# Cross-attention keys produced already turned, with their head norms applied to the scores

## The chip, the cores and the metric

The kernel runs on one core of a Trainium2 chip. The metric is the time of one execution in microseconds, the median of three runs. TensorE (PE) multiplies and turns tiles and writes PSUM; VectorE (DVE) and ScalarE (ACT) work on PSUM and SBUF; GpSimd (POOL) works on SBUF only; SyncE (SP) issues most transfers. The engines run their own instruction streams in order and meet through semaphores.

## The reference, cut to what matters

One block of a perceiver: cross-attention, a second attention without softmax, a mixture of experts. Only the cross-attention is touched. There are 32 sequences of 32 queries and 257 context rows, width 512, 8 heads of 64.

```
q = heads(layernorm(x) @ Wq);  k, v = heads(context @ Wkv)
q = per_head_ln(q) * qn_w;     k = per_head_ln(k) * kn_w     # (t-mean)*rsqrt(var+1e-6), over the head's 64
attn = softmax(where(mask, q @ k^T / 8, -inf));  out = (attn @ v) @ Wo
```

The kernel takes the mean out of the weights (each head's columns are centred), so a head norm is one multiply by rsqrt(mean of squares + eps). Both norm weights and the 1/8 are put on the queries.

## The kernel before, in words

**Precision.** A fp32 product is made of three fp32r products: both operands are split into a high part (ScalarE copy) and a low part (difference), and `split_products` (L23) issues high x high, high x low, low x high for each of 4 chunks of 128 of the contraction. All these matmuls carry the line L32.

**The loop.** `batch` (one in each engine's program) is one step b = 1 to 32, run in a register loop over tiles of 4 steps (r = 0 to 3). Step b finishes sequence b-1 and prepares b and b+1. The order on every engine is written out by hand. TensorE in step b:

1. scores of sequence b-1 (L1682): 8 products, keys of one head (64 rows) by 32 queries, on eight different 64x32 tiles of the array, into pS (2 banks);
2. turns of context b+1 (L1539), 8 transposes into the banks pT0 and pT1 (`pTT`);
3. second half of the keys of b: `k_half`, 12 products of 512 columns into pK1. The stationary operand is the turned context of 128 rows, so keys come out with a context row per partition;
4. the output tile of the last four sequences (L1638), in steps with r = 1 only, from step 5 on;
5. first half of the keys of b+1 into pK0, first 9 of its 12 products;
6. turns of the probabilities of b-1 (L1712), then the last 3 products of 5; with r = 0 also the turns of the last context row's probabilities (L1720);
7. turns of the normalised keys of b (L1730), 8 transposes into the same banks as 2;
8. products of context and probabilities (24 of 256 columns, into pP, then pV1; in the trace pP and pV by L32). Values are never made: the probabilities are applied to the context, and the weights come in 4.

VectorE in step b: masked scores (L1153, `s_m`), their maximum (L1156), the two low parts of context b+1 (L1033), four small operations for the softmax's divisor (L1164 to L1172), sum of squares and normalising of key half 1 (`k_sum` L1038, `k_norm` L1044), the low part of the turned probabilities (L1183), the last key column (L1190), the copy of turned keys (L1083), sum and normalising of the next key half 0, and the z copy (L1199).

ScalarE in step b: high part of context b (L768), high parts of the turned context b+1 (L668), two exponentials (L776), square of key half 1 (L676), scaling of the probabilities (L783), `k_root` (a Ln and an Exp of 8 columns, L680, L682), high part of the turned probabilities (L794), copy of turned keys (L672), square of the next half 0, a z copy (L814), again `k_root`; with r = 0 also four copies for the last row (L821).

GpSimd makes the context's low part (L541) and copies the queries (L547), in steps 30 and 31 also a low part of the attention output (L578). SyncE loads the context two steps ahead.

In front of the loop, eight query tiles are made; the keys of sequence 0 and half of those of 1 are made among them and after them, then the value product of the last context rows (L1623).

Of the kernel before, what the change touches and what calls it, by code (L numbers as in the profile page):

```python
# [15 lines left out]
P = 128  # L16
# [20 lines left out]
def perceiver_block(nc, x, ctx, mask, xWq, xWkv, xWo, qn_w, kn_w, aWq, gq, bq, mq, vq, aWk, gk, bk, mk, vk,  # L37
# [34 lines left out]
    with ExitStack() as es:  # L72
# [18 lines left out]
        def sem(name):  # L91
# [65 lines left out]
        kn_x = at("kn_x", [P, 3, D], 82 * KB)  # L157
# [9 lines left out]
        kn = at("kn", [P, 2, D], 113 * KB + 8320)  # L167
        p_rem = at("p_rem", [P, G, 3, B], 117 * KB + 8320)
# [104 lines left out]
        k_mm, k_sq, k_ss, k_lg, k_rs, k_n, k_t, kT0_set, kT1_set, k_rem = (sem(n) for n in (  # L273
            "k_mm", "k_sq", "k_ss", "k_lg", "k_rs", "k_n", "k_t", "kT0_set", "kT1_set", "k_rem"))
# [88 lines left out]


# [4 lines left out]
        def _(sp):  # L369
# [59 lines left out]
            sp.wait_ge(k_t, B * MT)  # L429
# [213 lines left out]
        def _(act):  # L643
# [26 lines left out]
            def keys_copy(n):  # L670
                act.wait_ge(k_t, (n - 1) * MT + 1)
                act.activation(kT[:, :, 0:P], pTT[0][:, :, :], ACT.Copy).then_inc(kT0_set, 1)  # L672

            def k_square(b, t):
                act.wait_ge(k_mm, b * MT + t + 1)
                act.activation(sq[:, t], pKV[t][:, :], ACT.Square).then_inc(k_sq, 1)  # L676
# [26 lines left out]
            for t in range(TILES):  # L703
# [38 lines left out]
                if t in (6, 7):  # L742
                    n = t - 6
                    act.wait_ge(k_mm, n + 1)
                    act.activation(sq_x[:, :], pC[1 - n], ACT.Square).then_inc(k_sq, 1)
                    act.wait_ge(k_ss, n + 1)
                    act.activation(head_log[:, 2], head_ss[:, 2], ACT.Ln, bias=HEAD_B, scale=1.0 / HD).then_inc(k_lg, 1)
                    act.wait_ge(k_lg, n + 1)
                    if n == 0:
                        act.wait_ge(rem_dve, 2)  # L750
                    else:
                        act.wait_ge(k_n, 1)
                    act.activation(head_rs[:, 2], head_log[:, 2], ACT.Exp, scale=-0.5).then_inc(k_rs, 1)
                if t == TILES - 1:
                    act.wait_ge(rem_pe, 3)
                    act.activation(kT_rem[:, :, :], pAV[0][:, :, 0:B], ACT.Copy).then_inc(rem_act, 1)
                    keys_copy(1)
            k_square(1, 0)
            k_root(1, 0)

            def batch(tile, r, main=True, prev=True, nxt=True, first=False):
# [25 lines left out]
                if main:  # L787
                    k_root(b, 1)
# [13 lines left out]
                if main:  # L802
                    keys_copy(b + 1)
# [11 lines left out]
                if nxt:  # L815
                    k_root(b + 1, 0)
# [179 lines left out]
        def _(dve):  # L996
# [39 lines left out]
            def k_sum(b, t):  # L1036
                dve.wait_ge(k_sq, b * MT + t + 1)
                nc.vector.tensor_reduce(head_ss[:, t], heads(sq[:, t]), AX.X, ALU.add).then_inc(k_ss, 1)  # L1038

            def k_norm(b, t, reused=True):  # L1040
                dve.wait_ge(k_rs, b * MT + t + 1)
                if reused:
                    dve.wait_ge(k_t, b * MT + t - 1)
                tt(heads(kn[:, t]), heads(pKV[t][:, :]), per_head(head_rs[:, t]), ALU.mult).then_inc(k_n, 1)  # L1044

# [35 lines left out]
            def keys_copy(n):  # L1081
                dve.wait_ge(k_t, n * MT)
# [891 lines left out]
```

## Time and profile before

| | us |
|---|---|
| median of 3 runs | 746.81 (746.39 to 746.88) |
| the profiled execution | 746.33 |
| its span, first to last instruction | 744.5 |
| TensorE busy | 712.8 (96%) |
| TensorE weight loads | 591.7 (79%) |
| VectorE busy | 490.5 (66%) |
| ScalarE busy | 441.3 (59%) |
| GpSimd busy | 239.4 (32%) |

The granted TensorE clock is 0.994 of full speed over the span. Busy times overlap. A TensorE row's length holds the modelled end of its last product; the pace is read from start to start. In the timeline a row may merge several instructions of one kind (xN); an entry in brackets says how long the engine stood idle before, and for whom.

### The profile page before, as it was taken

The numbers are of one execution on the slowest core, as the hardware profiler recorded it, in microseconds if no ns is written. First come the engines' busy times: TensorE is split into PE (matmuls) and PEld (weight loads), VectorE is DVE, ScalarE is ACT, GpSimd is POOL, SyncE is SP. The second block draws the span as 40 slices with busy tenths as digits, with TensorE's granted clock in tenths as the row PEclk, the third lists the DMA queues.
The fourth block names the chain that finished last, engine by engine and source line by source line (L and its number), as shares of the span: only waits on it lengthen the run. The fifth ranks groups of instructions, "written<-read, shape, count | busy, mean of one in ns | idle before, by whom it ended". The sixth has DMA issues, their size and how long they took to land.

```text
span 744.5 us, 14137 instructions
## 1 busy us (share of the span) xinstructions
PE 712.8 (96%) x4901; PEld 591.7 (79%) x4901; DVE 490.5 (66%) x903; ACT 441.3 (59%) x958; POOL 239.4 (32%) x208
## 2 busy tenths in 40 slices
PE   4899999999999999999999999999999969999995
PEld 3677888888888888888888888788778847888874
DVE  6766776775756757757667676867367875655573
ACT  4655775675766656756657675564655335655650
POOL 1462211221211212221212143753830023555525
PEclk9999999999999999999999999999999999999998
DMA  9931121212121212112212305630115447665658
GB/s 303 104 129 42 44 87 44 85 42 71 55 85 42 85 42 84 43 58 69 84 43 85 100 2 167 201 119 38 58 48 200 136 171 238 112 103 105 111 83 322
DMA packets 59672, 75.21 MB, mean 101 GB/s; under 512 B 8784, under 2 KB 33360, under 8 KB 59632
## 3 DMA queue, kind: packets, MB, share of 16 engines
q1 hardware_dynamic: 52032, 58.16, 26.0%
q0 software_dynamic: 4720, 11.27, 8.2%
q10 hardware_dynamic: 2880, 5.24, 2.0%
q8 instruction: 24, 0.39, 0.2%
q14 instruction: 16, 0.13, 0.1%
HBM read 54.75 MB, written 19.92 MB: 100 GB/s over the span
## 4 chain that ended last, share of the span: by engine, by line
PE 85%; DVE 6%; DMA 3%; ACT 2%; issue 2%; POOL 1%; SPq 0%; POOLq 0%; DVEq 0%
PE pK L32 41%; PE pV L32 11%; PE pP L32 9%; PE pV L1638 5%; PE pT L1539 4%; PE pT L1730 4%; PE pS L1682 2%; PE pP L1712 2%; PE pT L1877 1%; DMA fin<-total 1%; PE pT L1519 1%; DMA big<-x_rows,idx_x 1%; PE pS L1807 1%; DMA total<-big,idx 1%; PE pS L1900 1%
## 5 line engine op out<-in xcount | busy, mean ns | idle before, releaser
L32 PE MATMUL pK<-parts 128*128 128x512 f32 x744 | 187.8, 399 | 0.0
L541 POOL TENSOR_TENSOR parts<-big,parts 128x1024 fp32r<-128x1024 f32 x32 | 77.9, 2434 | 309.3 <-ACT parts L768 309.3
L32 PEld LDWEIGHTS pK<-parts 128*128 128x128 f32 x744 | 134.4, 188 | 27.0 <-issue 1.2
L1044 DVE TENSOR_TENSOR kn<-pK,head_rs 128x512 f32<-128x512 f32 x62 | 42.9, 692 | 58.0 <-ACT head_rs L682 58.0
L32 PE MATMUL pK<-w,lhs 128*128 x276 | 69.2, 399 | 0.9 <-issue 0.5
L32 PEld LDWEIGHTS pK<-w,lhs 128*128 128x128 f32 x276 | 50.3, 188 | 12.2 <-issue 2.5
L1465 DVE TENSOR_TENSOR w_p<-big,w_p 128x1024 fp32r<-128x1024 f32 x22 | 27.0, 1225 | 37.7 <-ACT w_p L959 37.7
L32 PE MATMUL pP<-pT,parts 128*128 128x256 f32 x384 | 51.6, 283 | 0.1
L616 POOL DMA_INDIRECT big<-x_rows,idx_x x23 | 26.7, 1162 | 73.7 <-DVE idx_x L1421 59.4
L1038 DVE TENSOR_REDUCE head_ss<-sq 128x8 f32<-128x512 f32 x62 | 42.5, 685 | 11.4 <-ACT sq L676 11.4
L676 ACT ACTIVATE sq<-pK 128x512 f32<-128x512 f32 x62 | 36.8, 594 | 21.4 <-PE pK L32 21.3
L32 PEld LDWEIGHTS pP<-pT,parts 128*128 128x128 f32 x384 | 46.3, 188 | 3.8 <-issue 1.8
L32 PE MATMUL pV<-pT,parts 128*128 128x256 f32 x384 | 49.1, 277 | 0.0
L794 ACT ACTIVATE pT<-pP 128x512 fp32r<-128x512 f32 x32 | 19.1, 598 | 48.9 <-PE pP L1712 48.8
L32 PE MATMUL pK<-w_p,parts 128*128 128x512 f32 x168 | 44.1, 412 | 3.7 <-DVE parts L1017 3.3
L32 PEld LDWEIGHTS pV<-pT,parts 128*128 128x128 f32 x384 | 46.2, 188 | 0.0
L622 POOL DMA_INDIRECT total<-big,idx x20 | 31.7, 1586 | 41.1 <-ACT big L973 41.1
L1183 DVE TENSOR_TENSOR pT<-pP,pT 128x512 fp32r<-128x512 f32 x32 | 22.1, 692 | 30.5 <-ACT pT L794 30.5
L32 PEld LDWEIGHTS pK<-w_p,parts 128*128 128x128 f32 x168 | 31.7, 195 | 12.2 <-DVE parts L1017 4.1
L1033 DVE TENSOR_TENSOR parts<-pT,parts 128x512 fp32r<-128x512 f32 x62 | 39.7, 681 | 2.2 <-ACT parts L668 2.2
L32 PE MATMUL pK<-w_a,xT_hi 128*128 128x512 f32 x128 | 40.1, 395 | 0.0
L768 ACT ACTIVATE parts<-big 128x1024 fp32r<-128x1024 f32 x31 | 32.7, 1053 | 6.6 <-PE pV L32 6.6
(330 smaller groups left out, 1523.0 us busy)
## 6 DMA issues: line engine op xcount, KB each, us to landing
big<-in_ctx_dram SPq DMA_DIRECT2D x32, 512.0 KB, 3.9
total<-zero SPq DMA_DIRECT2D x32, 256.0 KB, 4.1
w_raw<-in_L_ffn_w_dram SPq DMA_DIRECT2D x16, 512.0 KB, 6.1
big<-in_L_ffn_w_dram SPq DMA_DIRECT2D x8, 512.0 KB, 4.0
fin<-total SPq DMA_DIRECT2D x8, 512.0 KB, 7.8
x_rows<-big ACTq DMA_DIRECT2D x8, 256.0 KB, 2.1
total<-big ACTq DMA_DIRECT2D x8, 256.0 KB, 2.3
big<-in_x_dram SPq DMA_DIRECT2D x1, 1536.0 KB, 10.2
```

Of the source, the lines that this page charges most:

```text
L32: last = pe.matmul(out, lhs(a, c), rhs(b, c), start=start and c == first and n == 0, stop=stop and c == chunks - 1 and n == 2)
L541: nc.gpsimd.tensor_tensor(ctxN[:, u, LO], ctx_raw[:, u], ctxN[:, u, HI].bitcast(F32), ALU.subtract).then_inc(cn_lo, 1)
L622: nc.gpsimd.indirect_dma_start(total[:, :], bass.IndirectOffsetOnAxis(idx[:, j:j + 1], 0), y_sb[:, j % 2, :], None, bounds_check=5 * T - 1 ...
L676: act.activation(sq[:, t], pKV[t][:, :], ACT.Square).then_inc(k_sq, 1)
L768: act.activation(ctxN[:, u, HI], ctx_raw[:, u], ACT.Copy).then_inc(cn_hi, 1)
L1033: tt(ctxT[:, u, LO, :, t * P:(t + 1) * P], pTT[t][:, :, :], ctxT[:, u, HI, :, t * P:(t + 1) * P].bitcast(F32), ALU.subtract).then_inc(ctx_ ...
L1038: nc.vector.tensor_reduce(head_ss[:, t], heads(sq[:, t]), AX.X, ALU.add).then_inc(k_ss, 1)
L1044: tt(heads(kn[:, t]), heads(pKV[t][:, :]), per_head(head_rs[:, t]), ALU.mult).then_inc(k_n, 1)
L1465: tt(w2_buf(j)[:, LO], w2_all[:, bass.ds(e, 1)].rearrange("p e c n -> p (e c) n"), w2_buf(j)[:, HI].bitcast(F32), ALU.subtract).then_inc(w ...
L1539: last = pe.transpose(pTT[t][:, c, :], ctx_raw[:, u, t, c * P:(c + 1) * P], ident[:, :])
L1638: last = pe.matmul(o, weights, rows[:, e * C + c].rearrange("p b q -> p (b q)"), start=k == 0, stop=k == C, tile_position=(0, e * HD))
L1730: last = pe.transpose(pTT[t][:, c, :], kn[:, t, c * P:(c + 1) * P], ident[:, :])
```

## The change

The keys' product is turned round: a chunk of 128 weight columns is the stationary operand, all 256 turned context rows move. The keys come out with the head's dimension on the partitions, as the scores need them: half 0 (heads' chunks 0 and 1) in pK0, half 1 in pK1. They are copied to kT without norm. Their squares are multiplied by ones (which hold 1/512) on the tiles of the scores; this puts each head's mean of squares into pS where the scores will be, per query row and key. ScalarE makes the roots, `key_rs`, and VectorE multiplies the scores by them before the mask. The last context row's keys keep their old way. `k_sum`, `k_norm` and the key turns go.

```diff
+        key_rs = at("key_rs", [P, G, MT * P], 113 * KB + 8320)
+        half_keys = lambda buf, h: buf.rearrange("p (j m) -> p j m", j=2)
...
-            sp.wait_ge(k_t, B * MT)
             sp.wait_ge(p_t, B)
@@ ScalarE @@
-            def k_root(b, t):
-                act.wait_ge(k_ss, b * MT + t + 1)
-                act.activation(head_log[:, t], head_ss[:, t], ACT.Ln, bias=HEAD_B, scale=1.0 / HD).then_inc(k_lg, 1)
-                act.wait_ge(k_lg, b * MT + t + 1)
-                act.activation(head_rs[:, t], head_log[:, t], ACT.Exp, scale=-0.5).then_inc(k_rs, 1)
+            def keys_copy(b, src):
+                act.activation(kT[:, 0:2, 0:MT * P], half_keys(src, 0), ACT.Copy).then_inc(kT0_set, 1)
+            def k_square(b, h):
+                act.wait_ge(k_mm, b * 2 + h + 1)
+                act.wait_ge(ss_mm, b)
+                act.activation(sq[:, h], pKV[h][:, :], ACT.Square).then_inc(k_sq, 1)
+            def k_root(b, used=True):
+                act.wait_ge(ss_mm, b + 1)
+                if used:
+                    act.wait_ge(sc_s, b)
+                act.activation(key_rs[:, :, :], pS[:, :, 0:MT * P], ACT.Ln, bias=HEAD_B, scale=float(D // HD)).then_inc(ss_lg, 1)
+                act.wait_ge(ss_lg, b + 1)
+                act.activation(key_rs[:, :, :], key_rs[:, :, :], ACT.Exp, scale=-0.5).then_inc(k_rs, 1)
@@ ScalarE, batch @@
                     act.activation(ctxN[:, u, HI], ctx_raw[:, u], ACT.Copy).then_inc(cn_hi, 1)
+                    act.wait_ge(sc_mm, b)
+                    act.wait_ge(k_mm, b * 2 + 1)
+                    keys_copy(b, pKV[0][:, :])
                 if nxt:
                     ctx_high(b + 1, 1 - u)
...
-                if main:
-                    k_root(b, 1)
...
                 if main:
-                    keys_copy(b + 1)
+                    k_root(b)
                 if nxt:
                     k_square(b + 1, 0)
...
-                if nxt:
-                    k_root(b + 1, 0)
@@ VectorE, batch @@
                 if prev:
                     dve.wait_ge(sc_mm, b)
+                    dve.wait_ge(k_rs, b)
+                    tt(pS[:, :, 0:MT * P], pS[:, :, 0:MT * P], key_rs[:, :, :], ALU.mult).then_inc(sc_s, 1)
+                    dve.wait_ge(sc_s, b)
                     stt(s_m[:, :, 0:M], masked[:, bass.ds(p, 1), :].broadcast_to([P, G, M]), -BIG,
...
                 if main:
-                    k_sum(b, 1)
+                    dve.wait_ge(sc_mm, b)
+                    ts(kT[:, :, M - 1:M], kT_rem[:, :, bass.ds(b, 1)], 1.0, None, ALU.mult).then_inc(k_rem, 1)
+                    dve.wait_ge(k_sq, b * 2 + 2)
+                    keys_copy(pKV[1][:, :])
...
-                if main:
-                    k_norm(b, 1, reused=not first)
...
-                if main:
-                    dve.wait_ge(k_t, b * MT + 1)
-                    ts(kT[:, :, M - 1:M], kT_rem[:, :, bass.ds(b, 1)], 1.0, None, ALU.mult).then_inc(k_rem, 1)
-                    keys_copy(b + 1)
-                if nxt:
-                    k_sum(b + 1, 0)
-                if nxt:
-                    k_norm(b + 1, 0)
@@ TensorE @@
+            def key_products(bank, h, j, u, **part):
+                c = 2 * h + j
+                return split_products(pe, half_keys(bank, h)[:, j, :], weight(wkv, c * P, (c + 1) * P),
+                                      lambda s, k: ctxT[:, u, s, k, :], part.pop("chunks", C), **part)
+            def key_sums(b, squares):
+                pe.wait_ge(k_sq, b * 2 + 2)
+                pe.nop(nofuse=True)
+                for c in range(C):
+                    for e in range(2):
+                        half = slice(e * HD, (e + 1) * HD)
+                        last = pe.matmul(pS[c * S:(c + 1) * S, e, 0:MT * P], ones[half, 0:S],
+                                         half_keys(squares[half, c // 2, :], c // 2)[:, c % 2, :], start=True, stop=True,
+                                         tile_position=(e * HD, c * S))
+                last.then_inc(ss_mm, 1)
@@ TensorE, in front of the loop @@
-            pe.wait_ge(ctx_lo, 3)
-            key_turn(0)
-            split_products(pe, pK0[:, :], ctx_rows(1, 0), wk, C).then_inc(k_mm, 1)
-            pe.wait_ge(k_n, 2)
-            pe.wait_ge(ctx_lo, 4)
-            key_turn(1)
-            query_turn(TILES - 1)
+            query_turn(TILES - 1)
+            pe.wait_ge(ctx_lo, 4)
+            for j in range(2):
+                last = key_products(pK0[:, :], 0, j, 1)
+            last.then_inc(k_mm, 1)
+            pe.wait_ge(q_out, TILES)
+            key_sums(0, sq_first)
+            pe.wait_ge(kT1_set, 1)
@@ TensorE, batch @@
-                    if not first:
-                        pe.wait_ge(sc_m, b - 1)
+                    pe.wait_ge(ss_lg, b)
...
                 if main:
-                    pe.wait_ge(k_n, b * MT)
+                    pe.wait_ge(kT1_set, b)
+                    pe.wait_ge(k_sq, b * 2)
...
-                    k_half(b, 1, u)
+                    for j in range(2):
+                        last = key_products(pK1[:, :], 1, j, u)
+                    last.then_inc(k_mm, 1)
...
+                if main:
+                    pe.wait_ge(kT0_set, b + 1)
+                    pe.wait_ge(k_sq, b * 2 + 1)
                 if nxt:
-                    pe.wait_ge(k_n, b * MT + 1)
-                    pe.wait_ge(ctx_lo, b * MT + 3)
-                    split_products(pe, pK0[:, :], ctx_rows(1 - u, 0), wk, C - 1, stop=False)
+                    pe.wait_ge(ctx_lo, b * MT + 4)
+                    key_products(pK0[:, :], 0, 0, 1 - u)
+                    key_products(pK0[:, :], 0, 1, 1 - u, chunks=2, stop=False)
...
                 if nxt:
-                    split_products(pe, pK0[:, :], ctx_rows(1 - u, 0), wk, C, start=False, first=C - 1).then_inc(k_mm, 1)
+                    key_products(pK0[:, :], 0, 1, 1 - u, start=False, first=2).then_inc(k_mm, 1)
...
                 if main:
-                    pe.wait_ge(k_n, b * MT + 2)
...
-                    for t in range(MT):
-                        for c in range(C):
-                            last = pe.transpose(pTT[t][:, c, :], kn[:, t, c * P:(c + 1) * P], ident[:, :])
-                        last.then_inc(k_t, 1)
+                    pe.wait_ge(sc_m, b)
+                    key_sums(b, sq)
```

## Rows read from the trace of the kernel before

**Rows 1.** The page: busy us, share, instructions; the chain by line.
```profile
PE 712.8 (96%) x4901; PEld 591.7 (79%) x4901; DVE 490.5 (66%) x903; ACT 441.3 (59%) x958; POOL 239.4 (32%) x208
...
PE pK L32 41%; PE pV L32 11%; PE pP L32 9%; PE pV L1638 5%; PE pT L1539 4%; PE pT L1730 4%; PE pS L1682 2%; PE pP L1712 2%; PE pT L1877 1%; DMA fin<-total 1%; PE pT L1519 1%; DMA big<-x_rows,idx_x 1%; PE pS L1807 1%; DMA total<-big,idx 1%; PE pS L1900 1%
```

**Rows 2.** Timeline of TensorE in step 19: start us, length us, what.
```profile
290.00 0.66 PE L1682 MATMUL pS<-kT,q_b 64*32 64x257 f32 x16
290.59 1.09 PE L1539 MATMUL pT<-ident,big 128*128 128x128 f32 x8
291.44 5.05 PE L32 MATMUL pK<-parts 128*128 128x512 f32 x21
296.33 0.60 PE L1712 MATMUL pP<-ident,prob 128*128 128x128 f32 x4
...
297.46 1.04 PE L1730 MATMUL pT<-ident,kn 128*128 128x128 f32 x8
298.44 1.60 PE L32 MATMUL pP<-pT,parts 128*128 128x256 f32 x12
...
301.33 0.67 PE L1682 MATMUL pS<-kT,q_b 64*32 64x257 f32 x16
```

**Rows 3.** Timelines of TensorE in very short windows of the same step.
```profile
292.22 0.62 PE L32 MATMUL pK<-parts 128*128 128x512 f32 x2
...
295.88 0.62 PE L32 MATMUL pK<-parts 128*128 128x512 f32 x2
...
298.63 0.39 PE L32 MATMUL pP<-pT,parts 128*128 128x256 f32 x2
...
299.76 0.28 PE L32 MATMUL pP<-pT,parts 128*128 128x256 f32 x1
```

**Rows 4.** Timeline of VectorE and ScalarE in the same step.
```profile
289.84 0.69 DVE L1044 TENSOR_TENSOR kn<-pK,head_rs 128x512 f32<-128x512 f32 x1 [1.37 <-ACT head_rs L682]
...
290.45 0.68 DVE L1199 TENSOR_SCALAR z<-pV 128x512 f32<-128x512 f32 x1
...
291.05 0.68 DVE L1153 SCALAR_TENSOR_TENSOR s_m<-mask_f,pS 128x514 f32<-128x514 f32 x1
...
291.77 0.69 DVE L1156 TENSOR_REDUCE neg_max<-s_m 128x2 f32<-128x514 f32 x1
292.37 1.28 DVE L1033 TENSOR_TENSOR parts<-pT,parts 128x512 fp32r<-128x512 f32 x2
...
294.49 0.60 ACT L676 ACTIVATE sq<-pK 128x512 f32<-128x512 f32 x1 [0.90 <-PE pK L32]
294.98 0.90 ACT L783 ACTIVATE prob<-prob,p_scale 128x256 f32<-128x256 f32 x2
...
296.97 0.60 ACT L794 ACTIVATE pT<-pP 128x512 fp32r<-128x512 f32 x1 [0.59 <-PE pP L1712]
...
297.60 0.69 DVE L1183 TENSOR_TENSOR pT<-pP,pT 128x512 fp32r<-128x512 f32 x1 [0.49 <-ACT pT L794]
```

**Rows 5.** Timeline at the start of step 1 and of step 32.
```profile
66.35 0.67 PE L1682 MATMUL pS<-kT,q_b 64*32 64x257 f32 x16
...
67.19 0.69 DVE L1153 SCALAR_TENSOR_TENSOR s_m<-mask_f,pS 128x514 f32<-128x514 uint8 x1 [1.35 <-PE pS L1682]
...
451.72 0.66 PE L1682 MATMUL pS<-kT,q_b 64*32 64x257 f32 x16
...
451.82 0.69 DVE L1199 TENSOR_SCALAR z<-pV 128x512 f32<-128x512 f32 x1 [2.46 <-PE pV L32]
...
452.49 0.69 DVE L1153 SCALAR_TENSOR_TENSOR s_m<-mask_f,pS 128x514 f32<-128x514 uint8 x1
```

**Rows 6.** Timeline of GpSimd and VectorE in step 31.
```profile
444.07 1.30 POOL L578 TENSOR_TENSOR out_first<-qoT,out_first 128x512 fp32r<-128x512 f32 x1
...
444.42 0.97 DVE L1168 SCALAR_TENSOR_TENSOR p_scale<-neg_max,p_inv 128x2 f32<-128x2 f32 x1
```

**Rows 7.** Groups by line: a Ln of 512 columns: busy us, mean ns.
```profile
L826 ACT ACTIVATE bn_vec<-bn_vec,bias 128x512 f32<-128x512 f32 x2 | 1.4, 720 | 0.3 <-DMA bn_vec<-in_L_attn_vq_dram 0.3
```

More of the change, by code:

```diff
@@ L272, in perceiver_block @@
         ctx_t, ctx_hi, ctx_lo = sem("ctx_t"), sem("ctx_hi"), sem("ctx_lo")
[L273 to L274 removed]
+        k_mm, k_sq, ss_mm, ss_lg, k_rs, sc_s, kT0_set, kT1_set, k_rem = (sem(n) for n in (
+            "k_mm", "k_sq", "ss_mm", "ss_lg", "k_rs", "sc_s", "kT0_set", "kT1_set", "k_rem"))
         cn_hi, cn_lo = sem("cn_hi"), sem("cn_lo")
@@ L744, in _ @@
                     act.wait_ge(k_mm, n + 1)
[L745 to L748, printed above, removed]
+                    act.activation(sq_first[:, n], pC[1 - n], ACT.Square).then_inc(k_sq, 1)
                     if n == 0:
[L750 to L753, printed above, removed]
+                        keys_copy(0, pC[1])
                 if t == TILES - 1:
@@ L1597, in _ @@
                     pe.wait_ge(ctx_lo, 2)
-                    split_products(pe, pC[1], ctx_rows(0, 0), wk, C).then_inc(k_mm, 1)
+                    for j in range(2):
+                        last = key_products(pC[1], 0, j, 0)
+                    last.then_inc(k_mm, 1)
                 if t == 7:
@@ L1687, in batch @@
                 if main:
-                    pe.wait_ge(k_n, b * MT)
+                    pe.wait_ge(kT1_set, b)
+                    pe.wait_ge(k_sq, b * 2)
                     if first:
                         pe.wait_ge(q_n, TILES)
-                    k_half(b, 1, u)
+                    for j in range(2):
+                        last = key_products(pK1[:, :], 1, j, u)
+                    last.then_inc(k_mm, 1)
                 if r == 1 and not first:
                     out_tile(tile - 1)
+                if main:
+                    pe.wait_ge(kT0_set, b + 1)
+                    pe.wait_ge(k_sq, b * 2 + 1)
                 if nxt:
-                    pe.wait_ge(k_n, b * MT + 1)
-                    pe.wait_ge(ctx_lo, b * MT + 3)
-                    split_products(pe, pK0[:, :], ctx_rows(1 - u, 0), wk, C - 1, stop=False)
+                    pe.wait_ge(ctx_lo, b * MT + 4)
+                    key_products(pK0[:, :], 0, 0, 1 - u)
+                    key_products(pK0[:, :], 0, 1, 1 - u, chunks=2, stop=False)
                 if main and not nxt:
-                    pe.wait_ge(k_n, b * MT + 1)
                     project(0)
@@ L1724, in batch @@
                 if main:
-                    pe.wait_ge(k_n, b * MT + 2)
-                    if nxt:
-                        pe.wait_ge(ctx_lo, b * MT + 4)
-                    for t in range(MT):
-                        for c in range(C):
-                            last = pe.transpose(pTT[t][:, c, :], kn[:, t, c * P:(c + 1) * P], ident[:, :])
-                        last.then_inc(k_t, 1)
+                    pe.wait_ge(sc_m, b)
+                    key_sums(b, sq)
                 if prev:
```

58 lines of the change are left out of this document (15 added, 43 removed).

## The prediction

> **What bounds the kernel now.** I read three views in this order: the page's busy times and chain, the timeline of TensorE inside the cross-attention loop, and then the other engines in the same stretch. TensorE is busy 712.8 us of 744.5, and the chain of work that ended last runs through its products; the two lines that write pK, pV and pP lead it [rows 1]. So time is TensorE's program order plus what it waits for. A step of the loop (steps b = 1 to 32 score sequence b-1) repeats almost unchanged; rows 2 show step 19, from S = 290.00 to the next S at 301.33, 11.33 us. Its parts: scores 0.59, context turns 0.85, 21 key products 4.89, turns of the probabilities at T = S+6.33, 3 key products, 8 key turns, then the products of probabilities and context at T+2.11 until the next S, 2.89.
>
> The key turns start at 297.46 and would take what the 8 context turns take, 0.85; the next products start 0.98 later [rows 2]. They were waiting for a chain: T at 296.33, ScalarE's high part at 296.97, VectorE's low part at 297.60 for 0.69, TensorE at 298.44, so 0.15 from the end of that write to the product [rows 2, 4]. So T to T+2.11 is set by the other engines, and TensorE work removed there gives nothing. Before T, TensorE is the bound: ScalarE's scaling of the probabilities ends at 295.88, 0.45 before T [rows 4].
>
> **Key products, 24 of 512 columns become 48 of 256.** The order turns round (weights as stationary operand, turned context moving), so keys come out turned. Price from one stretch: the 4th product of 512 starts at 292.22 and the 20th at 295.88, 16 steps of 0.229. The 2nd of 256 columns starts at 298.63 and the 12th at 299.76, 10 steps of 0.113 [rows 3]. Two of 256 cost 0.226, a hair less than one of 512. Before T: 42 x 0.113 + 0.08 for the first (0.19 between first and second, 298.44 to 298.63) = 4.83 against 4.89, -0.06. The lower end of this cost is that -0.06, the upper end the mean over a whole block of them (298.44 to 301.33 is 24 in 2.89, 0.120 each [rows 2]), 42 x 0.120 + 0.08 = 5.12, +0.23. I take 0.113, since a block's excess sits in its first and last steps. The last 6 of the 48 lie behind T, where the chain hides them.
>
> The Trainium skill (TensorE: Matmul & The Clock Gate, section Back-to-back issue gap) gives a warm matmul N/2.4 ns plus a fixed 2.5 ns. By that, 24 more of them would cost an estimated 0.06 per step where the rows give -0.06. The rows decide, but a size rule that speaks against the change is kept as a rival.
>
> **Key turns out, sums of squares in.** The 8 turns go; 8 products of squares with ones come, on the same eight 64x32 tiles as the scores, one column fewer: 0.59 [rows 2]. Behind T TensorE now has 0.36 + 6 x 0.113 + 0.59 = 1.63 before the chain lets it go at 2.11: gain 0, and 0.48 of cover. Should the sums not run side by side on their tiles as the scores do (ends: 0.59 and 16 passes x 0.113 = 1.8, as each of the 8 shows two records), the excess over 0.48 would be 0.7 per step.
>
> **VectorE.** Per step, two reductions and two normalising multiplies go (one is the 0.69 at 289.84 [rows 4]); a copy of keys stays the same size and moves forward; one multiply of 128x512 of scores by the roots comes, PSUM in and PSUM out. Busy time falls about 4 x 0.69 - 0.69 = 2.1 us per step, off the chain. But the new multiply stands first in VectorE's queue, in front of mask, maximum and the two context low parts. And TensorE now wants both low parts for the next step's first key product, since a turned product spans all 256 rows; before, it wanted the first only. This is the step that decides, so I lay it out from S:
> - z copy: before, it started at S+0.45 because the normalising multiply held VectorE [rows 4]; with that gone it starts when the products end, S+0.10 to 0.15 (451.72 to 451.82, VectorE idle [rows 5]). The scores are readable at S+0.84 (66.35 to 67.19) or S+0.77 (451.72 to 452.49, behind the z copy) [rows 5]: multiply at S+0.80.
> - multiply to mask: a waited successor follows at 0.72 (291.05 to 291.77 [rows 4]). No row shows VectorE writing PSUM; ends 0.65 and 0.85, I take 0.74, nearest to the operations that read PSUM. Mask S+1.54, maximum 2.26, first low part 0.60 later 2.86, both end 1.28 later at 4.14, TensorE 0.15 later: S+4.29.
> - TensorE is free at 1.44 + 24 x 0.113 + 0.08 = S+4.23 (S to 291.44 is 1.44).
> So about 0.06 of new wait, and some of the 0.08 that a first product takes: 0.11 of stall against 0.06 gained, +0.05 per step. Ends: ready at 4.20, no stall, -0.06; ready at 4.45, +0.24.
>
> The Trainium skill (Perfetto Trace Analysis, section Optimizing Scalar/DVE Operations) puts VectorE's access overhead near 60 ns in SBUF and 125 ns in PSUM. By that, a PSUM destination would put the multiply's successor an estimated 0.06 later than the rows' 0.72. No row here shows it.
>
> **ScalarE.** Four 8-column roots per step become a Ln and an Exp of 512; such a Ln takes 0.72 [rows 7], Exp at most that. They run after the high part: sums end near T+1.65, Ln by T+2.6, Exp by T+3.3; the scores that wait for the Ln start at T+5.0, the multiply that waits for the Exp later still. Hidden, with 2.4 to spare. Its copy of the first key half goes in front of the context high parts and delays them by at most a copy's 0.60 (296.97); the low parts now come 0.5 later themselves. The exponentials end 1.13 after the maximum now (maximum to 292.46, ScalarE idle for 0.90 before 294.49), so at S+4.1 after the change; the square that stands behind them waits for the second key half and starts at S+4.49 as now, so the scaling ends at S+5.88 as now, under T [rows 4]. GpSimd's parts keep their place; SP's dropped wait for key turns precedes one for the probability turns that comes later, so it moves no load.
>
> **The ends.** Steps 30 and 31 are different: there GpSimd computes low parts of the output (444.07, 1.30 us) and a small VectorE operation stands still until they end (444.42, 0.97 us [rows 6]). The two in front of it now get through before; with VectorE's chain 0.5 later all three queue behind it, 0.5 later, and the slack of 0.3 under T goes: +0.35 each, +0.7. At the front, two groups of 4 turns go (-0.85), the sums come (+0.59), three key blocks save 0.04 each: -0.3; the roots lie behind the value product of the last row.
>
> **Sum.** 22 steps with r = 0, 2 or 3: 22 x 0.05 = +1.1. The 8 steps with r = 1 have the output tile (or, in step 1, a free VectorE) as cover: 8 x -0.06 = -0.5. Ends +0.7 - 0.3 = +0.4. Together +1.0 on the profiled execution of 746.33 (its span is 744.5, 1.8 lie around it and stay), 747.3; the median of the runs, 746.81, is 0.48 above it, so 747.8 as a median. A change is measurable here from about 0.2%, 1.5 us: I forecast no measurable change.
>
> **Rivals.**
> 1. The context low parts decide (slower). If the multiply cannot start before S+1.05, where the mask starts now, all of VectorE's chain is 0.25 later, ready is 4.54, the stall 0.31 + 0.08, and 22 x 0.33 + 0.4 - 0.5 = +7: 754. It decides from ready = S+4.3; each 0.1 costs 2.2. For it: 0.06 of nominal stall is already there. Against: what holds VectorE until S+0.45 is removed. Chance 0.30, most of it with halfway values, 749 to 752.
> 2. No stall (faster). Ready under 4.23: 30 x -0.06 - 0.3, with or without the ends' 0.7: 744.7 to 745.4. For it: margins within the rows' own scatter. Chance 0.22.
> 3. Smaller products cost more each. At the 0.120 of whole groups, TensorE is free at 4.40, which hides the stall; 22 x 0.23 + 8 x 0.2 + 0.4 = +7: 754; half of it, 750. Against it: ten even steps of 0.113. Chance 0.07.
> 4. The sums run one after the other on their tiles: 31 x 0.7 = +22, 768. The scores on the same tiles speak against it. Chance 0.02.
> Forecast, within 1.5 us of 746.8: 0.39.
>
> **How the numbers follow.** Time 747.8. The range leaves out rival 4, the top of 1 and 3 and little below: 744.4 to 753.0. Faster 0.22, same 0.39, slower 0.39.
>
> **What would show it.** Right: the 21-product block becomes 42 in about 4.83 plus a gap of 0.1 after the 24th; T to the next product stays 2.1; VectorE's busy time falls by some 65 us with no gain in span. Wrong: the multiply of scores starts later than S+0.9 or holds the mask longer than 0.8; a product of 256 columns steps at more than 0.115; the sums take over 1.1; the interval from S to S leaves 11.2 to 11.5.

## The result and the profile after

The changed kernel takes 756.27 us in the median of 4 runs (754.61 to 757.34) beside 746.85 for the kernel before on the same chip: 1.0114 times as long, 95% interval 1.0093 to 1.0134. The prediction was 747.8, within 744.4 to 753.0, and no measurable change: the kernel is slower by 9.4 and lies outside the range. The profiled execution took 755.76, its span 754.0, 9.5 more than the 744.5 of before.

First the page: busy times, the chain by line, and two groups. They answer to [rows 1].

```profile
PE 717.9 (95%) x5925; PEld 617.3 (82%) x5925; DVE 426.6 (57%) x807; ACT 447.3 (59%) x894; POOL 239.6 (32%) x208
...
PE 80%; DVE 9%; ACT 4%; DMA 3%; issue 2%; POOL 0%; SPq 0%; POOLq 0%; DVEq 0%; ACTq 0%
...
L32 PE MATMUL pK<-parts 128*128 128x256 f32 x1488 | 195.4, 287 | 0.9 <-DVE parts L1032 0.9
...
L1167 DVE TENSOR_TENSOR pT<-pP,pT 128x512 fp32r<-128x512 f32 x32 | 22.1, 691 | 64.4 <-ACT pT L795 64.4
```

VectorE lost 63.9 us of work and the span grew all the same. The 1488 key products waited for VectorE 0.9 us in the whole execution, all of it in step 4 (below), so for the rest their own pace or TensorE's order is the place to look, not a stall.

Next the timeline of TensorE in step 19, which answers to [rows 2].

```profile
295.52 0.67 PE L1665 MATMUL pS<-kT,q_b 64*32 64x257 f32 x16
296.11 1.09 PE L1516 MATMUL pT<-ident,big 128*128 128x128 f32 x8
296.96 5.28 PE L32 MATMUL pK<-parts 128*128 128x256 f32 x42
302.07 0.60 PE L1700 MATMUL pP<-ident,prob 128*128 128x128 f32 x4
302.43 0.96 PE L32 MATMUL pK<-parts 128*128 128x256 f32 x6
303.32 0.66 PE L1525 MATMUL pS<-sq,ones 64*32 64x256 f32 x16
304.18 1.60 PE L32 MATMUL pP<-pT,parts 128*128 128x256 f32 x12 [0.20 <-DVE pT L1167]
305.62 1.52 PE L32 MATMUL pV<-pT,parts 128*128 128x256 f32 x12
307.07 0.66 PE L1665 MATMUL pS<-kT,q_b 64*32 64x257 f32 x16
```

The 42 key products take 5.11 from start to start where 21 of 512 took 4.89. (S is the start of a step's scores, T that of its turns of the probabilities.) Behind T this step is as before: T to the next products 2.11, those 1.44 and 1.45. The step is 11.55 against 11.33. Two records inside the block, from very short windows, give the pace of one product, as in [rows 3]:

```profile
296.96 0.48 PE L32 MATMUL pK<-parts 128*128 128x256 f32 x2
...
299.32 0.40 PE L32 MATMUL pK<-parts 128*128 128x256 f32 x2
```

The second product starts at 297.16; the start at 299.32 is 18 products on: 2.16, 0.120 each, with no gap after the 24th. The granted clock does not tell the key block from the other: a table by stretch (busy us of each engine, then PEclk, DMA share, GB/s) has full speed, 2.4 GHz, for both.

```profile
297.20:301.90 4.70, 4.70 (x42) 4.70 (x41) 3.95 (x10) 3.43 (x9) 2.22 (x2) 1.00 0.30 76
304.40:307.00 2.60, 2.60 (x24) 2.54 (x23) 0.00 (x0) 1.98 (x4) 0.00 (x0) 1.00 0.00 0
```

Last, VectorE and ScalarE in the same step, which answer to [rows 4]:

```profile
295.62 0.69 DVE L1174 TENSOR_SCALAR z<-pV 128x512 f32<-128x512 f32 x1 [3.15 <-PE pV L32]
296.29 0.70 DVE L1134 TENSOR_TENSOR pS<-pS,key_rs 128x512 f32<-128x512 f32 x1
297.12 0.69 DVE L1136 SCALAR_TENSOR_TENSOR s_m<-mask_f,pS 128x514 f32<-128x514 f32 x1
298.45 1.28 DVE L1032 TENSOR_TENSOR parts<-pT,parts 128x512 fp32r<-128x512 f32 x2
300.61 0.90 ACT L786 ACTIVATE prob<-prob,p_scale 128x256 f32<-128x256 f32 x2
304.09 0.69 ACT L687 ACTIVATE key_rs<-pS,bias 128x512 f32<-128x512 f32 x1 [0.78 <-PE pS L1525]
304.81 0.63 ACT L689 ACTIVATE key_rs<-key_rs 128x512 f32<-128x512 f32 x1
```

The multiply starts at S+0.77, the mask 0.83 later, the low parts end at S+4.21. TensorE comes to the 25th key product, the first that needs the second low part, at S+4.40. Before, 0.15 passed from such a write to the product; by that it could start from S+4.36, so VectorE's chain is in time, by a few hundredths of a microsecond.

Step by step over the whole loop (starts of scores in both traces), the 9.5 us of span come from:

| where | us |
|---|---|
| T later, 21 ordinary steps, that is r = 0, 2, 3 without steps 4, 31 and 32 (S+6.56 for 6.34) | +4.7 |
| T later, 8 steps with r = 1 (11.28 for 11.09; step 1 6.54 for 6.30) | +1.6 |
| products of probabilities and context, 0.118 instead of 0.113 each in more steps (18 of 31, before 6) | +1.1 |
| step 4 (T at S+7.68 for 6.47) | +1.2 |
| T to those products, in steps with r = 0 | -0.2 |
| front; step 31 up to those products; after the last scores | +0.1, +0.2, +0.8 |

Step 4 is a stall of its own. Its timeline:

```profile
102.00 1.28 DVE L1195 TENSOR_TENSOR w_p<-big,w_p 128x512 fp32r<-128x512 f32 x2
102.73 3.11 PE L32 MATMUL pK<-parts 128*128 128x256 f32 x24
103.20 0.69 DVE L1134 TENSOR_TENSOR pS<-pS,key_rs 128x512 f32<-128x512 f32 x1
105.38 1.28 DVE L1032 TENSOR_TENSOR parts<-pT,parts 128x512 fp32r<-128x512 f32 x2
106.71 1.46 PE L32 MATMUL pK<-parts 128*128 128x256 f32 x10 [0.87 <-DVE parts L1032]
```

Low parts of the output weights stand in VectorE's queue before the multiply, once, and the 25th key product waits 0.87 for the context's second low part. The last step has a smaller case of the same. There T is 0.34 later (S+6.51 for 6.17); without the multiply (a_nomul below) it is at S+6.17 again. So 0.3 of the 0.8 after the last scores is the multiply's.

### The profile page after: what moved, and what is told of

Read it like the earlier page. It is cut to its first block, busy times and chain, and to the rows that moved or that the text cites. A ratio compares the mean times of both kernels' runs of the same rounds, so it can differ in the third digit from the quotient of the medians.

```text
span 754.0 us, 16109 instructions
## 1 busy us (share of the span) xinstructions
PE 717.9 (95%) x5925; PEld 617.3 (82%) x5925; DVE 426.6 (57%) x807; ACT 447.3 (59%) x894; POOL 239.6 (32%) x208
## 4 chain that ended last, share of the span: by engine, by line
PE 80%; DVE 9%; ACT 4%; DMA 3%; issue 2%; POOL 0%; SPq 0%; POOLq 0%; DVEq 0%; ACTq 0%
PE pK L32 40%; PE pV L32 11%; PE pP L32 9%; PE pV L1622 5%; PE pT L1516 4%; PE pS L1665 2%; DVE pT L1167 2%; ACT pT L795 2%; PE pP L1700 2%; PE pT L1860 1%; DMA fin<-total 1%; PE pT L1494 1%; DVE bst L1001 1%; PE pS L1790 1%; DMA total<-big,idx 1%
## 5 line engine op out<-in xcount | busy, mean ns | idle before, releaser
L32 PE MATMUL pK<-parts 128*128 128x256 f32 x1488 | 195.4, 287 | 0.9 <-DVE parts L1032 0.9
L32 PEld LDWEIGHTS pK<-parts 128*128 128x128 f32 x1488 | 182.5, 192 | 2.7 <-issue 1.6
L1174 DVE TENSOR_SCALAR z<-pV 128x512 f32<-128x512 f32 x32 | 22.1, 692 | 100.8 <-PE pV L32 100.8
L779 ACT ACTIVATE prob<-s_m,neg_max 128x257 f32<-128x257 f32 x64 | 32.2, 507 | 13.2 <-DVE neg_max L1139 13.1
```

Of the source, the lines that this page charges most:

```text
L32: last = pe.matmul(out, lhs(a, c), rhs(b, c), start=start and c == first and n == 0, stop=stop and c == chunks - 1 and n == 2)
L779: act.activation(prob[:, g, 0:M], s_m[:, g, 0:M], ACT.Exp, bias=neg_max[:, g:g + 1], accum_out=p_sum[:, g:g + 1]).then_inc(sc_exp, 1)
```

## Experiments

The runs with an interval were executed four times or more; a_224, a_192, a_w64, a_nomul, a_pt0 and the five with traded or zeroed operands once each, so of them the traces count more than the times.

The theory after the result: a key product of 256 columns costs 0.120, and two of them more than one of 512 (0.229), whatever the new roles of the operands do. Rival: the new order (context moving, the multiply, the sums, the wait for both low parts) costs it.

### Size alone

b_split256 is the kernel before with every key product cut in two; operands keep their roles:

```
-split_products(pe, pKV[t][:, :], ctx_rows(u, t), wk, C)
+for n in range(2):
+    split_products(pe, pKV[t][:, n * 256:(n + 1) * 256], ctx_rows(u, t), weight(wkv, n * 256, (n + 1) * 256), C)
```

> The kernel before, with each key product of 512 columns made as two of 256 and nothing else changed (context still stationary). Theory 'small products step at 0.120 us in the key block, whichever operand is stationary': the turns of the probabilities start at S+6.55 in steps with r=0,2,3 instead of 6.33, the whole costs 30 x 0.2 = 6 us, some 753. Theory 'the turned roles (weights stationary, context moving) cost it': the products step at 0.113 as those of probabilities and context do, the turns start at S+6.3, 746 to 747.

Measured: 755.58 (755.15 to 757.1), 1.0116 times the kernel before, interval 1.0094 to 1.0138. Its timeline in step 19:

```profile
294.90 0.67 PE L1684 MATMUL pS<-kT,q_b 64*32 64x257 f32 x16
...
296.34 5.28 PE L32 MATMUL pK<-parts 128*128 128x256 f32 x42
301.46 0.60 PE L1715 MATMUL pP<-ident,prob 128*128 128x128 f32 x4
```

T is at S+6.56, as in the changed kernel, and summed over steps 1 to 30 without step 4 the later T costs 6.2 us in both. So the cut alone makes the key block as long as the whole change does, whichever operand moves. That the totals agree too is in part luck. In step 4 T is 0.1 later here and 1.2 in the changed kernel; in return b_split256 ran the products of probabilities and context at 0.118 in 24 steps (+1.8, not +1.1), started them 0.3 later behind T in all, not 0.2 earlier, and lost 1.1 after the last scores, not 0.8.

Is it the columns, or a price per product? Three variants of the changed kernel, each leaving part of the keys out: 224 or 192 moving columns, or 64 stationary columns.

```
-half_keys(bank, h)[:, j, :], weight(wkv, c * P, (c + 1) * P), lambda s, k: ctxT[:, u, s, k, :]
+half_keys(bank, h)[:, j, 0:224], weight(wkv, c * P, (c + 1) * P), lambda s, k: ctxT[:, u, s, k, 0:224]   # 0:192
+half_keys(bank, h)[0:64, j, :], weight(wkv, c * P, c * P + 64), lambda s, k: ctxT[:, u, s, k, :]
```

> The changed kernel with 224 instead of 256 columns in every key product (the keys of the last 32 rows of a sequence are left out). If the columns set the pace, a product steps at 0.120 x 224/256 = 0.105 and the turns start at S+5.95. If the issue of a load and a product, or the load of 128 columns, sets it, a product still steps at 0.120 and the turns stay at S+6.56.

> The changed kernel with 192 columns in every key product (the keys of 64 of 256 rows are left out). With 224 a product stepped at 0.112 instead of 0.120, less than the columns would give (0.105). If a floor of load or issue lies there, 192 columns step at 0.111 again and the steps with r=1 keep T at S+10.93. If the pace is columns plus a growing rest, they step near 0.100 and T there comes at S+10.4.

> The changed kernel with 64 instead of 128 stationary columns in every key product (half of the keys of each chunk are left out), 256 moving columns as before. If the load of the stationary operand sets the pace of 0.120, a product now steps at 0.107 to 0.110 and the key block of 42 takes 4.6 instead of 5.1; the turns then start when ScalarE or the context allow, S+6.2 to 6.35. If each product costs its columns plus a fixed part that has nothing to do with the load, it stays at 0.120 and S+6.56.

Measured: 749.55, 750.78 and 754.99. With 224 columns the pace is 0.112, and with 192 it is 0.112 too: 32 columns off 256 bring 0.008, the next 32 nothing. With both shorter ones T is S+6.32 to 6.39 in ordinary steps, held by the context's low part: with TensorE faster, VectorE's chain decides, at S+4.3, where the prediction had put it.

64 stationary columns leave 0.120 in ordinary steps (T at S+6.57). In the steps with r = 1, from step 9 on, all 42 products ran at 0.114 (in steps 1, 4 and 5 the last 18 of them did). The first and second part of the key block in step 21, in the changed kernel, then in a_w64:

```profile
320.17 3.11 PE L32 MATMUL pK<-parts 128*128 128x256 f32 x24
327.74 2.43 PE L32 MATMUL pK<-parts 128*128 128x256 f32 x18
```

```profile
319.34 2.98 PE L32 MATMUL pK<-parts 128*64 128x256 f32 x24
326.79 2.27 PE L32 MATMUL pK<-parts 128*64 128x256 f32 x18
```

So the stationary operand's width does not set the pace of an ordinary step, but it is not without effect. Whether that is its load is open.

### The other terms

a_nomul leaves the multiply of the scores out (they stay unnormalised, and ScalarE's next Ln waits for the mask in its place); a_low4 moves the output weights' low part from step 4 to step 28:

```
-tt(pS[:, :, 0:MT * P], pS[:, :, 0:MT * P], key_rs[:, :, :], ALU.mult).then_inc(sc_s, 1)      # a_nomul
-output_weight_low((0, 1))                                                                   # a_low4
-output_weight_low((2, 3))
+output_weight_low((0, 1, 2, 3))
```

> The changed kernel without the multiply of the scores by the roots (left out, so the scores are not normalised; the wait for the roots stays). Theory 'products' pace': nothing moves in ordinary steps, turns at S+6.56, only step 4 gains (0.7 of its 1.1), 755. Rival 'VectorE's longer chain holds the key products': the turns come 0.1 to 0.2 earlier in ordinary steps, 750 to 752.

> The changed kernel with VectorE's two low parts of the output weights taken out of the front of step 4 and made with the other two in step 28. Theory: step 4 alone lost 1.1 us, since in front of the longer chain they held both low parts of the context, and TensorE waited 0.87 in the middle of its key products; it falls from 12.67 to 11.65 and the time by 1.0, to 755.2. Rival 'the loop's code coming in costs it': step 4 keeps its 12.67.

Measured: 753.31 with T at 6.56 in ordinary steps as before and at 6.83 in step 4; 755.8 (ratio 1.0107, interval 1.0089 to 1.0125) with step 4 down from 12.67 to 11.64. So in this kernel the multiply costs TensorE nothing but in step 4, where it stands behind 1.28 of other work, and 0.3 in the last step. The total of a_low4 shows no gain clear of noise where 755.2 was expected: in the profiled execution 22 instead of 18 steps had the 0.118 pace, and the part after the last scores was 2.0 us longer, for which I have no cause. The total of a_nomul fell by more than its 0.9 in step 4: 10 instead of 18 steps at 0.118, and 0.8 less after the last scores.

a_shift3 puts 9 instead of 6 key products behind T, in the changed kernel; b_shift1 puts 4 instead of 3 there in the kernel before (r = 1, 2, 3), as that kernel waits behind T too:

```
-key_products(pK0[:, :], 0, 1, 1 - u, chunks=2, stop=False)             # a_shift3
+key_products(pK0[:, :], 0, 1, 1 - u, chunks=1, stop=False)
-split_products(pe, pK0[:, :], ctx_rows(1 - u, 0), wk, C - 1, stop=False)   # b_shift1
+early = 9 if r == 0 else 8
+some_products(pe, pK0[:, :], ctx_rows(1 - u, 0), wk, C, 0, early)
```

> The changed kernel with three more key products behind the turns of the probabilities (9 instead of 6). They go into the 0.2 to 0.4 us in which TensorE waits for the turned probabilities' low part. Theory: turns at S+6.20, products of probabilities and context still 2.10 behind them (2.3 in steps with r=0), 22 x 0.36 + 8 x 0.2 = 9.5 us less than the changed kernel, 747. Rival 'the probabilities' chain binds in front too': ScalarE's scaling ends at S+6.0, turns not before S+6.15; gain under 8.

> The kernel before with one key product of 512 columns more behind the turns of the probabilities (4 instead of 3) in steps with r=1, 2, 3; nothing else. There TensorE waits 0.19 us for the low part of the turned probabilities. Theory 'T to the next products is set by ScalarE and VectorE': T comes 0.23 earlier, at S+6.10, the products still start 2.10 to 2.15 behind it, 22 steps x 0.18 to 0.23 = 4 to 5 us less, 742 to 743. Rival 'the scaled probabilities are not there yet': T stays at S+6.2 or later, gain under 2.

Measured: a_shift3 752.11, ratio 1.0062 (1.0043 to 1.0081); T fell to 6.20, T to the products rose to 2.19 (2.41 with r = 0), and their pace was 0.118 in steps 1 to 30: 4 us instead of the 9.5 expected. b_shift1 744.28, ratio 0.9961 (0.9949 to 0.9972): T 6.11, the next products 2.15 later. It gained 3 us instead of 4 to 5, with 18 steps at the 0.118 pace instead of 6. It beats both kernels, and shows that the idle time behind T was real.

### Why 0.120 here and 0.113 there

Both blocks run 24 or more products of 256 moving columns. The 0.113 was not the only pace of the second block even before the change: 6 of 31 steps ran it at 0.118, among them step 18, whose halves start 1.49 and 1.50 apart in place of 1.44 and 1.45:

```profile
287.01 1.65 PE L32 MATMUL pP<-pT,parts 128*128 128x256 f32 x12
288.50 1.57 PE L32 MATMUL pV<-pT,parts 128*128 128x256 f32 x12
290.00 0.66 PE L1682 MATMUL pS<-kT,q_b 64*32 64x257 f32 x16
```

First the operands trade places: in a_pvops the first 24 key products take the operands of the other block, in a_keyops the other block takes the key operands. Then one operand at a time, in that other block; then the key products with zeros. The cuts are shortened.

```
+split_products(pe, half_keys(pK1[:, :], 1)[:, j, :], ctxN columns, pT, MT)                          # a_pvops
-split_products(pe, o, lambda s, t: ctxN[:, 1 - u, s, t, c * P:(c + 1) * P], lambda s, t: pT[:, s, t, :], MT)
+split_products(pe, o, weight(wkv, c * P, (c + 1) * P), lambda s, k: ctxT[:, 1 - u, s, k, :], MT)   # a_keyops
     # a_keymov: only pT -> ctxT;  a_keystat: only ctxN -> weight(wkv, ...)
-act.activation(ctxT[:, u, HI, ...], pTT[t][:, :, :], ACT.Copy)                                      # a_zero
+act.activation(ctxT[:, u, HI, ...], pTT[t][:, :, :], ACT.Copy, scale=0.0)   # low part: subtract -> mult
```

> The changed kernel in which, from step 2 on, the first 24 key products of a step read the operands of the products of probabilities and context (context rows stationary, turned probabilities moving; half of the keys is left out, and each output gets two short groups of 6). Theory 'the place in the step sets the pace (what the other engines and transfers do, or what ran before)': they step at 0.120 as the key products did. Theory 'the operands and their places in memory set it': they step at 0.113, the 24 take 2.79 instead of 2.96, and steps with r=1 are 0.17 shorter.

> The changed kernel in which the 24 products of probabilities and context read the key products' operands (weights stationary, turned context moving; the context sums are left out). If the place sets the pace, the two groups of 12 still take 1.44 or 1.49 each. If the operands set it, they take 1.52 each (0.120 x 12 + 0.08) in every step, with no quicker steps among them.

> The changed kernel; the 24 products of probabilities and context keep their stationary operand (context columns) but take the turned context, the key products' moving operand, in place of the turned probabilities. If the moving operand sets the pace, the two halves of that block start 1.51 to 1.53 apart (0.120 each) in every step as with both operands swapped, a step is 11.70 and the span near 757. If the stationary operand sets it, the halves stay at 1.44 or 1.49, steps 11.55 or 11.65, the span near 754. The rows of before never showed the 0.120 in this block.

> The changed kernel; the 24 products of probabilities and context keep the turned probabilities as moving operand but take the key weights as the stationary one. If the stationary operand sets the pace: halves 1.51 to 1.53 apart, steps 11.70, span near 757. If the moving one: 1.44 or 1.49, span near 754. If it is both together or neither alone: a value between in this run and in its twin.

> The changed kernel with the turned context of the key products set to zero (the copy of the high part scales by 0, the low part is a product with it); the same instructions, sizes and order, the keys are zero. If the numbers that flow through TensorE have a part in the 0.120, the key products step at 0.113 or less and the turns of the probabilities start at S+6.27 or earlier, down to a wait for the context low part at S+4.3, and the span falls by up to 22 x 0.2 + 8 x 0.3 = 7, to 747. If the pace is set by place, addresses or sizes alone: 0.120, T at S+6.56, span within 1 of 754.

Measured: 754.58 and 759.09 beside 750.04 for the kernel before on the same chip, then 759.25, 755.18 and 756.01 beside 748.40. The key operands brought 0.120 into the other block in all steps (halves 1.51 and 1.53 apart, steps 11.70), and so did the moving one alone; the stationary one alone left 1.44 or 1.49. The other block's operands ran at 0.118 in the key block, neither the 0.120 nor the 0.113 expected. Zeros changed nothing: T 6.56. Timelines of that block with the key products' moving operand (a_keymov), then with their stationary operand (a_keystat):

```profile
305.65 1.67 PE L32 MATMUL pP<-parts 128*128 128x256 f32 x12 [0.20 <-DVE pT L1167]
307.16 1.60 PE L32 MATMUL pV<-parts 128*128 128x256 f32 x12
308.69 0.67 PE L1665 MATMUL pS<-kT,q_b 64*32 64x257 f32 x16
```

```profile
303.98 1.60 PE L32 MATMUL pP<-pT,parts 128*128 128x256 f32 x12 [0.20 <-DVE pT L1167]
305.42 1.52 PE L32 MATMUL pV<-pT,parts 128*128 128x256 f32 x12
306.87 0.67 PE L1665 MATMUL pS<-kT,q_b 64*32 64x257 f32 x16
```

So it is something of the moving buffer. Key products take both operands from one buffer, `parts`, on multiples of 128 bytes from the start of the layout; the turned probabilities lie in `pT`, 64 bytes off such a multiple. Three runs move addresses alone:

```
+base = (nc.sbuf_base + 63) // 64 * 64 + 64                               # a_base64, b_base64: all buffers
+pT = at("pT", [P, 2, MT, G * P], 102 * KB + 8192, F32R)                  # a_pt0: 8256 before
```

> The changed kernel with its whole on-chip buffer layout shifted up by 64 bytes: the turned context then starts 64 bytes off a multiple of 128, the turned probabilities on one; before it was the other way round. If the start address of the moving operand sets the pace, the two blocks trade places: key products 0.113, T at S+6.3 to 6.4 (bounded by the context low part at S+4.3), products of probabilities and context 0.120, their halves 1.52 and 1.53 apart; a step is then 11.45 to 11.5, the median 752 to 755. If the pace goes with something else of the operand (its writer, the distance of 4 KB between high and low part against 2 KB), nothing changes: T 6.56, 1.44 or 1.49, 756.

> The kernel before with the same shift of 64 bytes. Its key products move the weights (a multiple of 128 bytes now, 64 off after). If the address matters as above: products of 512 step at 0.222 to 0.226 in place of 0.229, T falls by 0.06 to 0.15 to 6.2 to 6.3, while the products of probabilities and context rise to 0.120 and cost 0.17 per step: median 746 to 750. If not, 746.9.

> The changed kernel with the turned probabilities alone 64 bytes lower, on a multiple of 128 bytes. Address: the halves of their block start 1.52 and 1.53 apart in all steps, a step is 11.70, the span near 757. Not the address: 1.44 or 1.49, 754.

Measured: 756.55 (1.0128, 1.0106 to 1.015), 747.23 (1.0007, 0.9993 to 1.0021), 758.41. Moving everything changed nothing, so my wording of it, the start of the moving operand, fell. Moving `pT` alone brought the 0.120 into its block in every step:

```profile
305.69 1.67 PE L32 MATMUL pP<-pT,parts 128*128 128x256 f32 x12 [0.20 <-DVE pT L1167]
307.20 1.60 PE L32 MATMUL pV<-pT,parts 128*128 128x256 f32 x12
308.73 0.67 PE L1665 MATMUL pS<-kT,q_b 64*32 64x257 f32 x16
```

What fits these address runs is the offset between the two operands: on the same offset within 128 bytes 0.120, 64 bytes apart less. (a_w64, with 64 stationary columns on the same offset, does not fit in its steps with r = 1; offsets other than 0 and 64 were not run.) The reverse edit puts the turned context 64 bytes off (the buffers above it move by 128), in the changed kernel and, with the edit of b_shift1, in the kernel before:

```
-ctxT = parts[:, 4 * C * D:6 * C * D]
+ctxT = parts[:, 4 * C * D + 16:6 * C * D + 16]
-ctxN = parts[:, 6 * C * D:8 * C * D]
+ctxN = parts[:, 6 * C * D + 32:8 * C * D + 32]
```

> The changed kernel with the turned context alone moved 64 bytes up against the key weights and the natural context (which, like all buffers above, keep their places relative to each other to a multiple of 128). If a product costs 0.120 where its stationary and its moving operand start on the same offset within 128 bytes and less where they start 64 apart, the key products step at 0.113 (or at the 0.118 that the operands of the other block took in this place): without another wait T would be S+6.27 (or 6.47), the context low part at S+4.3 holds it to 6.37 at the earliest; r=1 steps T at 10.96 (or 11.17). Over 21 ordinary and 8 steps with r=1 that is 21 x 0.09 to 0.19 plus 8 x 0.11 to 0.32, 3 to 6.5 us off 756.3: 750 to 753.5, of the slowdown of 9.5 a third to two thirds. If the offsets do not matter, T stays 6.56 and the median 756.

> The kernel before with the two edits that could help it: 4 instead of 3 key products behind the turns of the probabilities (run by itself: 744.3, T 6.11) and the turned context 64 bytes off the key weights. If the offsets matter for products of 512 columns too by the same 7 ns, 20 of them before T bring 0.14, T 5.97, no earlier than the end of the scaling at S+5.88 allows: 741 to 742.5 in the median. If they matter only for products of 256, T stays 6.11 and the median 744.3. Both would be faster than the kernels before and after.

Measured: a_ctx64 755.33 beside 748.14, ratio 1.0105 (1.0088 to 1.0121), an interval that overlaps that of the change: no gain clear of noise, where 750 to 753.5 had been expected. Two records of its key block in step 19:

```profile
295.62 0.51 PE L32 MATMUL pK<-parts 128*128 128x256 f32 x3
...
297.63 0.40 PE L32 MATMUL pK<-parts 128*128 128x256 f32 x2
```

17 products in 2.01 are 0.118 each, and T is 6.50: in ordinary steps the offset takes about a quarter of the 0.22 out of the key block, not all. With r = 1, from step 5 on, the 18 key products behind the output tile did reach 0.113, and T fell from 11.28 to 11.14. The products of 512 columns went the other way. The key block of b_shift1, then that of b_shift_ctx64 (line 43 is the product loop that starts in mid-chunk):

```profile
289.59 3.01 PE L32 MATMUL pK<-parts 128*128 128x512 f32 x12
292.44 1.98 PE L43 MATMUL pK<-parts 128*128 128x512 f32 x8
294.26 0.60 PE L1723 MATMUL pP<-ident,prob 128*128 128x128 f32 x4
```

```profile
291.99 3.04 PE L32 MATMUL pK<-parts 128*128 128x512 f32 x12
294.87 2.03 PE L43 MATMUL pK<-parts 128*128 128x512 f32 x8
296.74 0.60 PE L1723 MATMUL pP<-ident,prob 128*128 128x128 f32 x4
```

20 products take 4.75 instead of 4.67, T is 6.19 instead of 6.11, and the median 749.54, 1.0021 times the kernel before (1.0007 to 1.0035). The layout that helps products of 256 costs those of 512. Of the 4.9 by which its span exceeds that of b_shift1 the later T is 2.5; another 1.3 is the pace of 0.118 in 30 steps instead of 18, and 1.0 lies after the last scores.

## Why the prediction was wrong

**The step that failed is the price of a key product of 256 columns.** I took 0.113, ten even steps of [rows 3], for 42 products, -0.06 per step, and wrote that a block's excess over it sits in its first and last steps. That is so in the block where I read it. But it is a block with other buffers, and a price for "the same shape" did not carry: the key block runs at 0.120 and takes 5.11 for the 4.83 foretold, 0.28 more; set against the -0.06 of the forecast, T is 0.22 later. Three of my signs of being wrong came true with it: a pace over 0.115, a step of 11.55 where 11.2 to 11.5 had been named, and a mask 0.83 behind the multiply where 0.8 had. The pace was the upper end that I had named, +0.23, and rival 3 with a chance of 0.07 and 754 us. That it came out at that number is luck: the 0.120 quoted there is a mean over 24 products in 2.89, in which 22 stepped at 0.113. Nor did I look beyond step 19: six other steps had 0.118 in the very block that I read. The Trainium skill's rule (TensorE: Matmul & The Clock Gate, section Back-to-back issue gap), columns at 2.4 GHz plus 2.5 ns, had spoken for a loss, of 0.06 per step. The trace agrees in the sign, +0.22 at T, and not in the size: beyond the columns it shows 6 to 13 ns per product of 256 (0.107 at 2.4 GHz) and 15 ns per product of 512 (0.213).

The other steps of the prediction, in its order:

- **Behind T nothing gained.** Right: T to the next products 2.11 before, 2.11 after. The row of the sums of squares is 0.66 long, as that of the scores, so they run side by side on their tiles (rival 4 out). They began 0.21 later than laid out, behind six key products that took 0.89 for 0.68, and left 0.20 of the cover of 0.48.
- **VectorE.** Busy time -63.9 for the 65 foretold, without gain. Multiply at S+0.77 for S+0.80, mask 0.83 later for 0.74, low parts at S+4.21 for 4.14. The stall of 0.11 did not come, since TensorE reached that point only at S+4.40; a_224 shows it when TensorE is faster, as 0.16 at the 25th product in step 19. Rival 1, which held 0.30, did not happen in ordinary steps, but the slower products hid the chain: the ready time came out 0.07 later than laid out.
- **ScalarE.** Ln 0.69 and Exp 0.63, both hidden; the scaling ended at S+5.99 for 5.88, still under T.
- **The ends.** Mis-sized: step 30 cost its 0.22 like any other and step 31 0.12, with no 0.35 on top in either; the front gained nothing instead of 0.3 (its three terms add up to 0.38). Missed: step 4, +1.2, the very mechanism of rival 1 in one step, because I looked at step 19 and did not ask in which steps VectorE's queue holds other work before the multiply; and 0.3 in step 32.
- **Not in the sum:** the products of probabilities and context, untouched by the change, ran at 0.118 instead of 0.113 in 12 more steps, +1.1. What chooses between the two is open. One kernel had both paces in neighbouring steps, and one execution of each kernel was traced. Runs that leave this block and its addresses alone had 10 (a_nomul) to 24 (b_split256) such steps, so the +1.1 need not come from the change.

So the explanation that is shown: cutting products of 512 into 256 at this place makes T later by just as much as the change does, 6.2 of its 9.5 us, by itself (b_split256); the multiply's place in VectorE's queue is another 1.2 in step 4 (a_low4) and 0.3 in the last step (a_nomul). That the relative address of the operands is part of their pace is shown by a_pt0, in one execution but in all its steps, and in smaller measure by a_ctx64. That it is all of the difference is not: with the 64 bytes the key block stayed at 0.118 in ordinary steps. The +1.1 of the block behind T and the other 0.5 us after the last scores are unexplained; that last part took 293.3 us (a_keystat) to 295.6 (a_low4) in kernels whose code there is the same, 293.6 in the changed kernel and 292.8 in the one before.

## What to carry to other kernels

Two TensorE products of half the columns can cost more than the one that they replace, and the price must be read from products on the same buffers and in more than one step: beyond its columns a product of 256 took 13 ns in one block and 6 or 11 in another of equal shape. Here these few nanoseconds made 0.22 us in an ordinary step and 6.2 of the 9.5 us. Where an engine is freed of work off the path (64 us here), expect nothing, and look in the special steps of a loop, not only in an ordinary one, for what now stands in front of a new operation in its queue. Idle time behind a turn is filled by moving products past it: one product of 512 columns more there was worth 0.4% in the kernel before.

## What the runs showed of the hardware

- At 2.4 GHz (granted clock 1.00), a product of 128 stationary columns steps every 0.229 at 512 columns, 0.113 to 0.120 at 256, 0.112 at 224 and 0.112 at 192: the 32 columns below 224 gained nothing. 64 instead of 128 stationary columns left 0.120 in ordinary steps and took 0.114 in those with r = 1.
- Products of 128 stationary and 256 moving columns whose operands start on the same offset within 128 bytes took 0.119 to 0.120 in steps 1 to 30 of each kernel that had them so; 64 bytes apart 0.113 or 0.118. At 512 columns 64 bytes apart cost 0.233 instead of 0.229. Zeros in the moving operand changed nothing (a_zero).
- VectorE's multiply from PSUM into PSUM took 0.70, and its waiting successor started 0.83 after its start, against 0.72 where the destination is not PSUM.
